# Row-by-row fetches in every fourth group instead of every second, and the first sweep's weighting moved from ScalarE to VectorE

## The reference, cut to what matters

```python
# layer 0: one head of 128 channels; layer 1: four heads of 32
e  = leaky_relu(a_src[src] + a_dst[dst], 0.2)      # layer 1 adds a term of the edge's attributes
ex = exp(e - segment_max(e, dst)[dst])
out = segment_sum(ex * h[src], dst) / segment_sum(ex, dst)
# layer 2 needs segment_sum(edge_attr_128, dst); layer 3:
agg = segment_sum((x @ W_rel)[edge_type, src], dst)
```

## Time and profile before

| what | value |
|---|---|
| time, median of 3 runs (lowest to highest) | 9807.24 us (9797.97 to 9817.08) |
| span of the profiled execution | 9691.9 us |
| what lies around the span, by the median | 115.3 us |
| busy: POOL / DVE / ACT / PE | 4970.1 / 3381.8 / 1028.8 / 645.5 us |
| DMA | 1045.34 MB, mean 108 GB/s |

### The profile page before, as it was taken

The page is one execution under the profiler, slowest core; times in us unless marked ns, Lnnn a source line. Parts: engine busy times, 40 slices in busy tenths (PEclk is TensorE's granted clock), DMA queues, the critical chain, the costliest instruction groups (busy, mean ns, idle before and its releaser), DMA issues.

```text
span 9691.9 us, 57509 instructions
## 1 busy us (share of the span) xinstructions
PE 645.5 (7%) x2460; PEld 429.5 (4%) x2460; DVE 3381.8 (35%) x6204; ACT 1028.8 (11%) x3093; POOL 4970.1 (51%) x5237
## 2 busy tenths in 40 slices
PE   1100000000140000000000000580000000000000
PEld 1000000000140000000000000240000000000000
DVE  6555555555563222222222222761111111111113
ACT  1222222222120000000000000460000000000000
POOL 5766666666457444444444444216444444444445
PEclk7555555555565555555555555795555555555555
DMA  4456666666433222222222222452222222222222
GB/s 158 145 178 199 194 186 196 192 193 202 155 108 94 67 72 70 69 73 69 73 70 72 70 71 69 164 200 71 64 67 66 68 68 68 65 70 68 68 68 97
DMA packets 344911, 1045.34 MB, mean 108 GB/s; under 512 B 111529, under 2 KB 139564, under 8 KB 306594
## 3 DMA queue, kind: packets, MB, share of 16 engines
q1 hardware_dynamic: 157746, 670.54, 19.3%
q0 software_dynamic: 172192, 365.19, 14.8%
q10 hardware_dynamic: 14544, 5.93, 0.3%
HBM read 527.27 MB, written 513.96 MB: 107 GB/s over the span
## 4 chain that ended last, share of the span: by engine, by line
SPq 36%; issue 31%; DVE 14%; another core or an unknown queue 8%; PE 3%; POOL 3%; ACT 3%; ACTq 1%; DMA 1%; DVEq 0%; POOLq 0%
SPq L250 21%; SPq L249 7%; SPq L247 7%; DVE ps L1256 2%; DVE ps L1281 2%; POOL node_sums L1387 1%; DVE edge_rows L1286 1%; ACT edge_rows L1220 1%; DVE edge_rows L1264 1%; PE ps L2028 1%; ACTq L250 1%; DVE edge_logit L1356 1%; DVE feat_prod L1343 1%; DVE fine L592 1%
## 5 line engine op out<-in xcount | busy, mean ns | idle before, releaser
L1158 POOL DMA_INDIRECT edge_rows<-table_b,src_i x1523 | 1440.8, 946 | 1642.7 <-DMA sums_b<-edge_rows 1161.0
L2113 POOL DMA_INDIRECT edge_rows<-table_rel,rel_row x1523 | 1440.7, 946 | 1641.1 <-DMA sums_rel<-edge_rows 1096.3
L1158 POOL DMA_INDIRECT edge_rows<-table_a,src_i x1568 | 1485.0, 947 | 702.8 <-issue 487.3
L2197 DVE TENSOR_TENSOR edge_rows<-edge_rows,ps 128x1024 f32<-128x1024 f32 x195 | 237.9, 1220 | 2301.3 <-DMA edge_rows<-table_rel 2220.7
L1286 DVE TENSOR_TENSOR edge_rows<-edge_rows,ps 128x1032 f32<-128x1032 f32 (+1 forms) x390 | 484.2, 1241 | 962.5 <-remote 726.8
L1350 DVE TENSOR_TENSOR edge_rows<-edge_rows,ps 128x2112 f32<-128x2112 f32 (+1 forms) x99 | 230.9, 2332 | 1010.1 <-ACT ps L1223 961.8
L1220 ACT ACTIVATE edge_rows<-edge_rows,weight_decay 128x129 f32<-128x129 f32 x1560 | 493.6, 392 | 211.5 <-issue 211.3
L1281 DVE TENSOR_TENSOR ps<-edge_rows,ps 128x1032 f32<-128x1032 f32 (+1 forms) x390 | 485.6, 1245 | 8.6 <-issue 1.9
L1316 DVE TENSOR_TENSOR z<-edge_rows,dst_logit 128x16 f32<-128x16 f32 (+2 forms) x198 | 40.1, 203 | 1194.2 <-DMA edge_rows<-table_b 1171.4
L1223 ACT ACTIVATE ps<-weight_decay 128x128 f32<-128x128 f32 (+1 forms) x99 | 27.7, 280 | 3036.5 <-DVE weight_decay L1337 1562.8
L2144 ACT ACTIVATE ps<-keep 128x16 f32<-128x16 f32 x98 | 19.6, 201 | 2985.8 <-issue 1534.7
(11 more groups left out here) (296 smaller groups left out, 3207.3 us busy)
## 6 DMA issues: line engine op xcount, KB each, us to landing
sums_a<-edge_rows SPq DMA_DIRECT2D x98, 2064.0 KB
sums_b<-edge_rows SPq DMA_DIRECT2D x98, 1120.0 KB, 4.2
edge_rows<-in_ea SPq DMA_DIRECT2D x98, 1024.0 KB
sums_rel<-edge_rows SPq DMA_DIRECT2D x98, 1024.0 KB, 3.9
table_rel<-rel SPq DMA_DIRECT2D x98, 512.0 KB
edge_rows<-table_b SPq DMA_DIRECT2D x2880, 0.5 KB
edge_rows<-table_b ACTq DMA_DIRECT2D x2880, 0.5 KB
edge_rows<-table_rel ACTq DMA_DIRECT2D x2880, 0.5 KB
```

The source lines that it names most:

```text
L1158: e.indirect_dma_start(out=rows[:, s, i, 0:L.W], out_offset=None, in_=L.table, in_offset=bass.IndirectOffsetOnAxis(ap=src[:, at:at + 1], a ...
L2113: e.indirect_dma_start(out=rows[:, s, i, :], out_offset=None, in_=table_rel, in_offset=bass.IndirectOffsetOnAxis(ap=rel_row[:, at:at + 1], ...
```

## The change

Two edits. The first makes every fourth group a helped group (7, 11, ..., 95: 23 groups) instead of every second (7, 9, ..., 95: 45 groups). The second removes ACT's weighting of the first sweep with its two semaphores; ACT makes weights and decays in one activation into PSUM, as in the second sweep, and DVE multiplies the rows of a group by their weights in one instruction.

```diff
-    helped_b = every(2, 7)
+    helped_b = every(4, 7)
...
-        if H == 1:
-            weighted = sem(f"edges_{L.name}_weighted")
-            weight_exped = sem("edges_weight_exped")
...
-                    if H == 1:
-                        e.activation(at[:, 0, cols, :], at[:, 0, cols, :], ACT.Exp).then_inc(weight_exped.sem, 1)
-                        e.activation(factors[:, 1, cols, :], at[:, 1, cols, :], ACT.Exp).then_inc(exped.sem, 1)
-                        if part == 0:
-                            e.wait_ge(*weight_exped.at(g + 1))
-                            for i in range(first * GK, end * GK):
-                                done = e.activation(R[:, i, 0:NW], R[:, i, 0:NW], ACT.Copy, scale=wd[:, g % 2, 0, i, :])
-                            done.then_inc(weighted.sem, 1)
-                    else:
-                        e.activation(factors[:, :, cols, :], at[:, :, cols, :], ACT.Exp).then_inc(exped.sem, 1)
+                    e.activation(factors[:, :, cols, :], at[:, :, cols, :], ACT.Exp).then_inc(exped.sem, 1)
...
-                if H == 1 and g == 0:
-                    e.wait_ge(*weighted.at(1))
...
-                if H == 1:
-                    e.wait_ge(*weighted.at(g + 1))
...
-                    if H > 1 or part == 1:
-                        weights = wd[:, b, 0, cols, :] if H == 1 else factors[:, 0, cols, :]
-                        now = heads(R)[:, cols, :, :]
-                        t_weight = then(e.tensor_tensor(now, now, bc(weights.unsqueeze(3), [P, (end - first) * GK, H, C + 1]),
-                                                        ALU.mult))
-                        join_step.append(t_weight)
+                    weights = factors[:, 0, cols, :]
+                    now = heads(R)[:, cols, :, :]
+                    t_weight = then(e.tensor_tensor(now, now, bc(weights.unsqueeze(3), [P, (end - first) * GK, H, C + 1]),
+                                                    ALU.mult))
+                    join_step.append(t_weight)
```

## The result

The change made the kernel faster: 8839.18 us (8834.05 to 8863.47, 4 runs) against 9811.34 us (9797.97 to 9817.08, 4 runs), a ratio of 0.9013, 95% interval 0.8999 to 0.9027. The forecast was 8790. The profiled span is 8834.5 us, and the time of that execution 8840.2.

A forecast was written before the change was run, and what follows sets the result against it. The prediction took POOL's waits, for DVE in the first sweep and for stores behind row quarters in the others, to bound the kernel. Savings of 226 + 396 + 396 = 1018 us off 9807.2 gave 8790, range 8250 to 9300.

The forecast's parts named there:

- The reading of the second and third sweep: Second and third sweep: POOL waits for stores behind quarters of rows; 22 cycles of 110 and 107.5 us save 396 us each.
- The clearing: After POOL's long burst: rows stay slow while something that filled up empties; 7 us a cycle in the second sweep.
- the sum: Whole kernel: 226 us from the first sweep plus 396 from each of the other two, 1018 us saved.
- store of G-2 and its landing until POOL restarts: 4.5 us: Second sweep's cycle: after the second quarter, POOL restarts once group G-2's store is issued and landed, 4.5 us.
- The first sweep: First sweep: weighting moved to DVE saves 226 us, 196 from POOL's waits for DVE and 30 at the end.
- POOL becomes the bound: First sweep: DVE needs 15 us a group against POOL's 20.0 (16 x 1.25), so POOL sets the pace.
- The lower bound that I gave for the saving: First sweep: saving of 0 if DVE slows to 22.3 us a group.
- the 228 us: First sweep: POOL's idle time beyond its own pauses, read as waiting for DVE, 2.3 us in each of 98 groups.
- The third rival: First sweep: DVE becomes the bound through waits of its short instructions, 25 us a group, 9280 us in all; chance 0.10.
- The second rival: All sweeps: POOL becomes the bound, rows fitting beside 78.8 us of gathers a cycle, 7465 us in all; chance 0.08.
- the row of 4.0 us: Second sweep, kernel before: a row fetch takes 4.0 us beside gathers that don't pause; argument against the second rival.
- 115.3 us around the span: Whole kernel: the median stands 115.3 us above the profiled span of 9691.9, so savings are taken from 9807.2.

The follow-up runs named there:

- no_rows: Changed kernel with no row fetches at all, POOL gathering all 16 columns of every group: 7909.18 us, ratio 0.8167 to the kernel before.
- three_edits: Changed kernel with 12 gathers a group in the first sweep, no row fetches and 64-row gathers in the second, a MEMSET before each gather in the third: 7438.74 us.
- the second set: Follow-up runs on a chip of their own: kernel before 6984.39 us, changed kernel unaltered 7040.85 us, ratio 1.008; three variants of gathering ran there too.
- paced_fourth: Changed kernel with a MEMSET of 128x224 on POOL ahead of every gather of all three sweeps: 8264.47 us, ratio 0.8451 to the kernel before.
- first, third and fourth sets: Follow-up runs, each set on a chip of its own together with the kernel before, which took 9680.26, 9702.12 and 9774.85 us in them.

## Why the prediction was right, and where it was not

**The reading of the second and third sweep** held in its lengths, and in the third sweep in its causes too. The views had shown a store behind a quarter of rows; the changed profile has bursts of 47 and 16 by turns, and in the cycle shown quarters of 62 us (load included) and 34, 60 and 32 being forecast. The clearing was put at 7 us and took 7.7. The mean cycle is 110.4 us in the second sweep (21 from 3183.5 to 5502.0; forecast 110) and 106.4 in the third (21 from 6313.4 to 8547.6; forecast 107.5). 22 x (128.4 - 110.4) = 396 and 22 x (125.4 - 106.4) = 418, where 396 and 396 stood in the sum; the stages gained 439 and 422. The 43 us more in the second sweep lie outside the 22 cycles, in its first and last groups, which I had left as they were. One step failed in the second sweep: "store of G-2 and its landing until POOL restarts: 4.5 us". What came last there was DVE's addition, behind the exponentials and ACT's quarter, 7.2 us after the store; the sum had priced SP's stream alone. The rest of the cycle came out shorter by about these 2.7 us. That no_rows took the second and third stage down by 950 and 839 us against the kernel before confirms that the row fetches were what POOL's pauses came from.

**The first sweep** was mis-sized: -226 in the sum, -11 measured, and -9 and +6 us between kernels of one set (2274 and 2282 us in the first, 2280 and 2274 in the fourth). The step that failed is "POOL becomes the bound" at 20.0 us a group. The lower bound that I gave for the saving (nothing, if DVE slows to 22.3 us) is the value that came, but not for the reason given there. The 22.3 us stood in the profile of before and I read it as the sum of two causes, 16 x 1.25 and 2.3 us of waiting for DVE. three_edits shows it to be one: 16 x 1.40, since with 12 gathers and the same work on DVE a group takes 16.8 us (12 x 1.40). By this the 228 us in which POOL "waits for DVE" were the limit's time, showing at the place where it could (1568 x 0.15 = 235). With ACT's 16 copies gone it shows in DVE's chain; with the gathers paced it shows nowhere in DVE (13.5 and 6.7 us idle), and the group takes 22.7 us all the same, 16 x 1.42, which is now POOL's own pace.

**The third rival** had the place right, DVE's short instructions late where ACT's had been, and the price wrong: DVE's pace came out at the same 22.3, not at 25, because DVE was not what set it.

**The second rival** was given 0.08 and is what the second set shows. I argued against it from the row of 4.0 us, which is right for that trace and says nothing of the second set. The Trainium skill, DMA: Bandwidth & Descriptors, section SWDGE vs HWDGE vs iDMA, says that DMAs issued from SP and ACT are immune to the interference with which VectorE can hold up GpSimd's writing of descriptors. If that is taken as a rule for rows beside gathers, the 13.66 us for 32 rows agree with it, and the 49.51 us for 17 rows do not. No run shows that VectorE held these up, so they speak against the wider rule and not against the skill's sentence.

**From span to time.** I put 115.3 us around the span; a run's time is its span + 5.7 us (8840.2 and 8834.5), so the profiled execution of the kernel before must have been some 110 us quicker than the timed ones, and of the 115.3 us only some 6 lie around a span. Between the profiled spans the change took 857 us off where the sum said 1018: 215 less in the first sweep, 69 more in the other two, 15 less elsewhere. From 9807.2 to 8839.2 are 968 us. The forecast lies only 49 us from the median because those 110 us, and the 69 of the other two sweeps, made up for most of the first sweep's 215. That nearness is luck.

## What to carry to other kernels

When a group takes the same time in stretches with different work (22.4 us in three sweeps whose engines' work and stores differ), look for what they have in common before you explain each by its own waits: leave some of it out, and divide the time saved by what was left out. Idle time that moved from one engine to the next when work was moved was the sign of it here. And run the kernel before in every set: here it took 9680 to 9775 us in three and 6984 in one, and the change that gained 10% in the former lost 0.8% in the latter.

Of what ran, the kernel without row fetches is best where the slow pace is (0.8167, while paced_fourth has 0.8451); it wasn't run where the pace is absent; there, by an estimate from POOL's pace, giving all columns to POOL would cost 45 x 2 x 1.25 = 112 us over the kernel before.

## What the hardware showed that I had not expected

- A limit of 1.40 us for an indirect gather, by its count and not by its size (128 rows of 560 bytes, or 64 of them), in the first, third and fourth sets and the first measurement; in the second set 1.25 us, POOL's own pace, held over whole sweeps (320 gathers from 3200.9 to 3599.9).
- Gathers may run ahead of it for a while: 180 at 1.25 us in no_rows, in the second sweep as in the third. Only then does POOL itself slow, by 1.94 us gathers and by "issue" waits. Meanwhile the others pay: a row takes 0.4 us alone and 4.0 in a long burst, and DVE's chain has the waits of 1 to 3 us shown above.
- A MEMSET of 0.17 us ahead of each gather adds only 0.03 us to it: the pause of 0.30 us between gathers becomes 0.17 us of MEMSET and one of 0.16.
- What the limit is stays open. No experiment here varied it from inside a kernel. It was absent in one of the sets, each of which had another chip; whether the chip is the cause was not tested. Whether it would be there in an execution that no profiler records wasn't tried either, since every run's time here comes with its span.
